# Routing tokens to experts: places per two batches, rows sent in four groups, attention results stored by token

## The reference

```python
x = x + tanh(g_xattn) * attention(layernorm(x), ctx, mask, topk=32)   # 16 heads of 16
x = x + tanh(g_ffn) * moe(layernorm(x))

# moe: 8 experts, 2 choices a token, N = 4096 tokens, capacity = N / 8 * 1.25 = 640
probs = softmax(x_flat @ gate_w.T); top, idx = top_k(probs, 2); top = top / sum(top)
for k in range(2):
    onehot = (idx[:, k, None] == experts)
    pos = (cumsum(onehot, axis=0) - 1)[token, idx[:, k]]     # place among the earlier tokens of that expert
    valid = pos < capacity
    disp[idx[:, k], pos] += x_flat where valid                # a table of its own for each k
    out += where(valid, top[:, k] * expert(disp)[idx[:, k], pos], 0)
```

## Time and profile before

| | |
|---|---|
| median of 3 runs | 3430.61 us (3429.76 to 3431.26) |
| the profiled execution | 3430.36 us, of which the span is 3428.6 us |
| busy, share of the span | PE 80%, DVE 82%, ACT 57%, POOL 53% |
| mean granted TensorE clock | 0.931 |

### The profile page before, as it was taken

The page is one execution under the profiler, slowest core; times in us unless marked ns, Lnnn a source line. Parts: engine busy times, 40 slices in busy tenths (PEclk is TensorE's granted clock), DMA queues, the critical chain, the costliest instruction groups (busy, mean ns, idle before and its releaser), DMA issues. The chain is left out here.

```text
span 3428.6 us, 77423 instructions
## 1 busy us (share of the span) xinstructions
PE 2727.2 (80%) x23469; PEld 1888.0 (55%) x23470; DVE 2805.7 (82%) x20098; ACT 1970.0 (57%) x3382; POOL 1826.1 (53%) x1278
## 2 busy tenths in 40 slices
PE   7838888888888888888888888832713999999990
PEld 5514445454544445454545454521603999999990
DVE  6749999999999999999999999944713766667653
ACT  2228888888888888888888888820200222222220
POOL 1017777777777777777777777710153111111107
PEclk9969999999999999999999999965856999999995
DMA  6961121121121111211211212011222112211206
GB/s 204 253 178 32 32 51 42 32 62 32 32 61 32 44 50 32 62 32 32 62 32 39 55 32 61 3 30 33 92 74 92 55 64 69 69 66 68 67 28 193
DMA packets 141983, 220.41 MB, mean 64 GB/s; under 512 B 22432, under 2 KB 103584, under 8 KB 138496
## 3 DMA queue, kind: packets, MB, share of 16 engines
q1 hardware_dynamic: 116608, 171.43, 18.3%
q0 software_dynamic: 9472, 29.37, 2.8%
q10 hardware_dynamic: 15488, 14.68, 1.3%
HBM read 142.02 MB, written 73.40 MB: 63 GB/s over the span
## 5 line engine op out<-in xcount | busy, mean ns | idle before, releaser
L568 DVE MAX8 a_cand<-a_sc 128x8 f32<-128x43 f32 (+1 forms) x12288 | 1682.8, 201 | 42.8 <-ACT a_sc L506 42.6
L640 POOL TENSOR_SCALAR a_low<-a_sc,a_top 128x1024 bf16<-128x1024 f32 x512 | 1456.2, 2844 | 0.0
L513 ACT ACTIVATE a_ex<-a_ps_e,a_nmax 128x1024 f32<-128x1024 f32 x512 | 577.7, 1128 | 149.4 <-PE a_ps_e L418 149.4
L506 ACT COPY a_sc<-a_ps_s 128x1024 f32<-128x1024 f32 x512 | 531.5, 1038 | 187.5 <-PE a_ps_s L406 170.7
L520 ACT COPY a_exT<-a_ps_t 128x512 f32<-128x512 f32 x1024 | 552.5, 602 | 0.3 <-PE a_ps_t L439 0.3
L439 PEld LDWEIGHTS a_ps_t<-a_ident,a_ex 128*128 128x128 f32 x4096 | 478.2, 140 | 102.1 <-ACT a_ex L513 1.0
L439 PE MATMUL a_ps_t<-a_ident,a_ex 128*128 128x128 f32 x4096 | 529.8, 272 | 0.8 <-ACT a_exT L520 0.8
L427 PE MATMUL a_ps_c<-a_low,a_row_of 128*16 128x512 bf16 x1024 | 307.2, 382 | 255.6 <-POOL a_low L640 214.7
L416 PE MATMUL a_ps_e<-a_ks,a_qs 96*128 96x512 bf16 x1024 | 394.3, 385 | 0.0
L418 PE MATMUL a_ps_e<-a_low,a_lowest 128*128 128x512 bf16 x1024 | 390.1, 381 | 0.0
L1292 POOL TENSOR_TENSOR e_wl<-e_raw,e_wh 128x2048 fp32r<-128x2048 f32 x24 | 110.5, 4603 | 519.9 <-DVE e_wh L1429 519.9
(11 more groups left out here) (196 smaller groups left out, 4676.4 us busy)
## 6 DMA issues: line engine op xcount, KB each, us to landing
scr_v<-p_vp SPq DMA_DIRECT2D x32, 512.0 KB, 6.1
a_vs<-scr_v SPq DMA_DIRECT2D x32, 512.0 KB, 5.8
a_mask<-in_mask SPq DMA_DIRECT2D x32, 512.0 KB, 6.6
scr_k<-p_kp SPq DMA_DIRECT2D x96, 128.0 KB, 2.4
a_ks<-scr_k SPq DMA_DIRECT2D x32, 384.0 KB, 4.7
a_qs<-scr_q SPq DMA_DIRECT2D x192, 64.0 KB, 5.2
scr_disp<-a_zeros SPq DMA_DIRECT2D x32, 320.0 KB, 6.9
e_xin<-scr_disp SPq DMA_DIRECT2D x40, 256.0 KB, 2.7
```

What stands on the lines that cost most here:

```text
L506: nc.scalar.copy(sc[:, i % 4, :], ps_s[:]).then_inc(copied[u], 1)
L513: nc.scalar.activation(ex[:, s % 2, :], ps_e[:], ACT.Exp, bias=nmax[:, v, s:s + 1]).then_inc(expd, 1)
L568: ins = nc.vector.max(c[:, 8 + n:8 + n + 7 * CH + 1:CH], sc[:, i % 4, pl.cut[n]:pl.cut[n + 1]])
L640: nc.gpsimd.tensor_scalar(low[:, i % 2, :], sc[:, i % 4, :], top[:, u, i, pl.TOPK - 1:pl.TOPK], None, ALU.is_lt).then_inc(lowed, 1)
```

## The change

- **Layout.** `attn` is now ordered by token, 32 tiles of 256 columns. `attend` and `repair` write their columns to the place of the head. PE turns the rows straight from `attn`; POOL's `gather` and the buffer `ain` are gone. `norm` writes straight into `xn`, which PE reads too; `keep_rows` and the buffer `xs` are gone, with the waits that belong to them.
- **Places per group.** A group is two batches, 8 tiles. In the steps of batches 2, 4 and 6, DVE marks the group before after `choose` (`mark`), and after `norm` it works out its slots (`slots`). POOL adds the marks tile by tile into a running sum `sofar`, eight dependent additions. PE, at the end of its step, takes the counts within a tile and the sums up to a tile into one accumulation of two products (`places`). The last group follows the last batch.
- **Sends per group.** POOL issues the 16 sends of a group as soon as its slots are there, then waits for the marks of the next group.

```diff
@@ attend, normalise
-                    ins = nc.scalar.activation(attn[:, bass.ds(Gn, 1), j * DK:(j + 1) * DK].rearrange("p o d -> p (o d)"),
+                    ins = nc.scalar.activation(attn[:, Gn // (G * pl.QT) * pl.QT + Gn % pl.QT, (Gn // pl.QT % G * HG + j) * DK:(Gn // pl.QT % G * HG + j + 1) * DK],
@@ repair, tile on DVE
-                link(V.tensor_scalar(attn[:, I * QT + t, bass.ds(j * DK, DK)], ps_u[:, 0:DK], rden[:], None, ALU.mult))
+                link(V.tensor_scalar(attn[:, (I // G) * QT + t, bass.ds((I % G) * (HG * DK) + j * DK, DK)], ps_u[:, 0:DK], rden[:], None, ALU.mult))
@@ route, POOL
-            def gather(b, u, start):
...
-            def keep_rows(b, u):
...
-            pool.wait_ge(slots_done, 2)
-            for n in range(TT):
-                for k in range(K2):
...
+            nc.gpsimd.memset(sofar[:, 0], 0.0).then_inc(added, 1)
+            for g in range(NG):
+                pool.wait_ge(hot, g + 1)
+                for t in range(g * GT, (g + 1) * GT):
+                    pool.wait_ge(added, t + 1)
+                    nc.gpsimd.tensor_tensor(sofar[:, t + 1], sofar[:, t], onehot[:, t], ALU.add).then_inc(added, 1)
+                pool.wait_ge(slots_done, g + 1)
+                for t in range(g * GT, (g + 1) * GT):
+                    for k in range(K2):
+                        pool.indirect_dma_start(
+                            out=scr["disp"], out_offset=bass.IndirectOffsetOnAxis(ap=slot_to[:, t, k:k + 1], axis=0),
+                            in_=xn[:, t, :], in_offset=None, bounds_check=ROWS - 1, oob_is_err=False).then_inc(sent, 16)
             pool.wait_ge(sent, 16 * TT * K2)
@@ route, PE
-                    if t == 0:
-                        pe.wait_ge(a_in, b + 1)
...
-                                                 ain[:, u, t, k * P:(k + 1) * P], ident[:])
+                                                 attn[:, b * QT + t, k * P:(k + 1) * P], ident[:])
...
-                                                 xs[:, u, t, k * P:(k + 1) * P], ident[:])
+                                                 xn[:, b * QT + t, k * P:(k + 1) * P], ident[:])
...
+                if b and b % GB == 0:
+                    places(b // GB - 1)
+
+            def places(g):
+                pe.wait_ge(hot, g + 1)
+                pe.wait_ge(added, g * GT + GT)
+                if g:
+                    pe.wait_ge(picked, g)
+                tiles = slice(g * GT, (g + 1) * GT)
+                nc.tensor.matmul(ps_n[:, 0:GT * C], upto[:], onehot[:, tiles].rearrange("p t k e -> p (t k e)"),
+                                 start=True, stop=False)
+                nc.tensor.matmul(ps_n[:, 0:GT * C], ones[:], sofar[:, tiles].rearrange("p t k e -> p (t k e)"),
+                                 start=False, stop=True).then_inc(counted, 1)
...
-            nc.tensor.matmul(ps_n[:, 0:TT * K2 * E], upto[:], onehot[:].rearrange("p t k e -> p (t k e)"),
...
+            places(NG - 1)
@@ route, DVE
-                if not start:
-                    dve.wait_ge(xn_kept, b - 1)
...
-                    ins = nc.vector.tensor_scalar(xs[:, u, t, :], x1[:, b * QT + t, :], mv[:, u, t, 0:1],
+                    ins = nc.vector.tensor_scalar(xn[:, b * QT + t, :], x1[:, b * QT + t, :], mv[:, u, t, 0:1],
...
                     choose(b - 1, 1 - u, start and b == 1)
+                if b and b % GB == 0:
+                    mark(b // GB - 1)
                 norm(b, u, start)
+                if b and b % GB == 0:
+                    slots(b // GB - 1)
+
+            def mark(g):
+                n = slice(g * GT, (g + 1) * GT)
+                link(nc.vector.tensor_copy(chosen[:, n], which[:, n, 0:K2]))
+                for k in range(K2):
+                    ins = nc.vector.tensor_tensor(onehot[:, n, k, :], lane[:].unsqueeze(1).broadcast_to([P, GT, E]),
+                                                  chosen[:, n, k:k + 1].broadcast_to([P, GT, E]), ALU.is_equal)
+                ins.then_inc(hot, 1)
+
+            def slots(g):
...
+                link(V.tensor_scalar(first[:, n], chosen[:, n], float(K2 * CAP), None, ALU.mult))
+                link(V.tensor_scalar(first[:, n, 1], first[:, n, 1], float(CAP), None, ALU.add))
+                dve.wait_ge(hot, g + 1)
+                dve.wait_ge(counted, g + 1)
+                V.tensor_tensor(flat(place[:]), ps_n[:, 0:GT * C], flat(onehot[:, n]), ALU.mult).then_inc(picked, 1)
+                dve.wait_ge(picked, g + 1)
+                link(V.tensor_reduce(at[:, n], place[:], AX_X, ALU.add))
...
+                V.tensor_copy(slot_to[:, n], tmp[:, n]).then_inc(slots_done, 1)
...
+            mark(NG - 1)
+            slots(NG - 1)
+            V.tensor_copy(slot_from[:], first[:]).then_inc(slots_done, 1)
```

More of the change, by code:

```diff
@@ L876, in route @@
     B, QT, TT, D, E, KD = pl.B, pl.QT, pl.TT, pl.D, pl.E, pl.KD
-    GD = pl.HG * pl.DK
     CAP, K2 = pl.CAP, 2
     ROWS = E * K2 * CAP
+    GB = 2
+    GT = GB * QT
+    NG = B // GB
+    C = K2 * E
     attn, x1, slot_to, slot_from, weight = (keep[n] for n in ("attn", "x1", "slot_to", "slot_from", "weight"))
@@ L913, in route @@
         onehot = sb("r_onehot", [P, TT, K2, E])
-        before = [sb(f"r_before{i}", [P, TT, K2, E]) for i in range(2)]
-        place = sb("r_place", [P, TT, K2, E])
+        sofar = sb("r_sofar", [P, TT + 1, K2, E])
+        place = sb("r_place", [P, GT, K2, E])
         at = sb("r_at", [P, TT, K2])
@@ L929, in route @@
         made = sem("r_made")
-        a_in = sem("r_a_in")
-        xn_kept = sem("r_xn_kept")
         x_in = [sem(f"r_x_in{u}") for u in range(2)]
@@ L947, in route @@
         hot = sem("r_hot")
+        added = sem("r_added")
         counted = sem("r_counted")
@@ L950, in route @@
         e_out = sem("r_e_out")
+        picked = sem("r_picked")
         slots_done = sem("r_slots_done")
@@ L989, in _ @@
                                     pattern=[[1, P]], channel_multiplier=-1).then_inc(made, 1)
-            def gather(b, u, start):
-                if not start:
[L993 to L997, removed]
-            def keep_rows(b, u):
[L1000 to L1010, removed]
-            pool.wait_ge(slots_done, 2)
-            for n in range(TT):
-                for k in range(K2):
-                    pool.indirect_dma_start(
-                        out=scr["disp"], out_offset=bass.IndirectOffsetOnAxis(ap=slot_to[:, n, k:k + 1], axis=0),
-                        in_=xn[:, n, :], in_offset=None, bounds_check=ROWS - 1, oob_is_err=False).then_inc(sent, 16)
+            nc.gpsimd.memset(sofar[:, 0], 0.0).then_inc(added, 1)
[10 more added lines that the diff above has]
+                            in_=xn[:, t, :], in_offset=None, bounds_check=ROWS - 1, oob_is_err=False).then_inc(sent, 16)
             pool.wait_ge(sent, 16 * TT * K2)
@@ L1173, in step @@
                     choose(b - 1, 1 - u, start and b == 1)
+                if b and b % GB == 0:
+                    mark(b // GB - 1)
                 norm(b, u, start)
+                if b and b % GB == 0:
[8 more added lines that the diff above has]
+            def slots(g):
+                V = nc.vector
+                n = slice(g * GT, (g + 1) * GT)
+                flat = lambda ap: ap.rearrange("p t k e -> p (t k e)")
+                link(V.tensor_scalar(first[:, n], chosen[:, n], float(K2 * CAP), None, ALU.mult))
[5 more added lines that the diff above has]
+                link(V.tensor_reduce(at[:, n], place[:], AX_X, ALU.add))
+                link(V.tensor_scalar(valid[:, n], at[:, n], float(CAP), None, ALU.is_le))
+                link(V.scalar_tensor_tensor(out=tmp[:, n], in0=at[:, n], scalar=-1.0, in1=valid[:, n], op0=ALU.add,
+                                            op1=ALU.mult))
+                link(V.tensor_tensor(first[:, n], first[:, n], tmp[:, n], ALU.add))
+                link(V.tensor_scalar(tmp[:, n], valid[:, n], -float(1 << 20), float(1 << 20), ALU.mult, ALU.add))
+                link(V.tensor_tensor(tmp[:, n], tmp[:, n], first[:, n], ALU.add))
+                V.tensor_copy(slot_to[:, n], tmp[:, n]).then_inc(slots_done, 1)
             dve.wait_ge(w_in, 16 * 5)
@@ L1185, in _ @@
             V = nc.vector
[L1186 to L1190, removed]
-            link(V.tensor_tensor(tmp[:, :, 0], best[:, :, 1], best[:, :, 0], ALU.subtract))
-            V.memset(before[0][:, 0:1], 0.0).then_inc(e_in, 1)
@@ L1194, in _ @@
[L1194 to L1209, removed]
-            dve.wait_ge(e_out, 1)
-            link(V.scalar_tensor_tensor(out=tmp[:], in0=at[:], scalar=-1.0, in1=valid[:], op0=ALU.add, op1=ALU.mult))
-            link(V.tensor_tensor(first[:], first[:], tmp[:], ALU.add))
@@ L1213, in _ @@
[L1213 to L1217, removed]
+            mark(NG - 1)
+            slots(NG - 1)
+            V.tensor_copy(slot_from[:], first[:]).then_inc(slots_done, 1)
+            dve.wait_ge(slots_done, NG + 1)
```

(7 more changed lines are left out.)

7 lines of the change are left out of this document (removed).

## The result

The changed kernel takes 3384.9 us, the median of four runs (3382.64 to 3386.18), against 3430.94 us of the kernel before in four runs beside it: a ratio of 0.9863 with a 95% interval of 0.9848 to 0.9878. The prediction said 3386. All medians and ratios here are of fast runs: one run of half_sends (7246.61 us) and one of the kernel before (6633.46 us, beside one_pool) took about twice as long and are left out. The profiled execution took 3385.42 us, its span is 3383.4 us, 45.2 less than the 3428.6 before.

A forecast was written before the change was run, and what follows sets the result against it. POOL's 64 sends, issued alone after the batches, bound the kernel; four rounds of 27.4 us plus 3 x 1.1 from 2433.3 end issue at 2546.2 instead of 2590.2, so 3430.4 − 44 gives 3386 us, range 3376 to 3400.

The forecast's parts named there:

- the first signal: In the routing batches, DVE's first marks are ready for POOL and PE at 2433.3 us.
- the four stretches from signal to first send: In each of POOL's four rounds, additions, count, slots and the start of sending take 6.9 us.
- the four bursts: POOL's 16 sends per round take 20.5 us, plus 1.1 us in the three rounds with batches beside them.
- The sums: Eight dependent additions per group on POOL: 0.35 us each, 2.8 us, bounds 1.5 and 3.9 us.
- The stretch: Sends beside a busy DVE in the batches cost 1.1 us more per 16 sends.
- Rival 1: Sends beside the batches wait for DVE's operations and take 1.66 us each: 15 us more, 3401 us; chance 0.14.
- rival 2: POOL and DVE exclude each other altogether in the batches, a pair takes 45.5 us: slower, 3437 us; chance 0.03.
- The batches' loss: PE stops at the count, delaying the next residual by 6.7 us in batches 2, 4 and 6: 20 us.
- POOL's 2546 ends last: At the end of issue, POOL's chain ends at 2546 us, the batches' at 2542, so only POOL's counts.
- a tie: In the routing stage, a pair of batches takes 27.9 us and POOL's round 28.5 us.
- Taken at nothing: Effects given no time; in the repair, five tiles' register work hides in DVE's 1.5 us waits, under 0.5 us uncovered.
- Rival 3: Short round: additions 1.5 us, no stretch, early PE, batches lose 4.5 us per pair, round under 26: 3376 us; chance 0.11.

The follow-up runs named there:

- half_sends: The changed kernel with only the first choice's sends in groups 0 to 2, 24 of 64 sends left out: 3381.5 us.
- one_pool: The changed kernel with one-batch groups, count and slots a step later, the first six groups' sums on POOL a group ahead, the last two on DVE: 3369.0 us.
- adds_dve: The changed kernel with the eight running sums of each group on DVE behind the marks instead of on POOL: 3380.5 us.
- places_later: The changed kernel with running sums on DVE, marks at the end of a step, and count and slots in the next step: 3376.5 us.
- layout_only: The kernel before with only the new layout by token, places worked out once and all 64 sends at the end: 3431.8 us.
- tail_busy: The changed kernel with 13 unused copies and 8 unused two-input operations on DVE beside the last 16 sends: 3386.28 us in one run.

## Why the prediction was right

**The mechanism and its size.** 48 sends went beside the batches at their old price, 16 stayed, and the end of issue came at 2544.9 us where 2546.2 was forecast. The parts, by the ledger of POOL's chain: the first signal came 3.2 us late (2436.5 for 2433.3); the four stretches from signal to first send took 6.34, 6.18, 6.18 and 6.12 us, 24.8 instead of 27.6; the four bursts 81.4 instead of 85.3; and POOL waited 2.2 us that the forecast had not. 2546.2 + 3.2 − 2.8 − 3.9 + 2.2 = 2544.9. The forecast is better than its terms: by luck, a late start and an added wait cancelled two terms that were too large.

**The sums** (forecast 2.8 us) took 2.4 us, 0.30 each. The rest of the round, 3.8 us from the sums' end to the first send, was forecast as 1.2 + 1.9 + 0.97 = 4.1.

**The stretch** (forecast 0.07 us a send in three bursts) was 1.311 − 1.277 = 0.03 us in the first burst, 0.02 in the second and none in the third. Rival 1, a send at 1.66 us, falls. So does rival 2: it decides at 2.27 us on average, and even back-to-back copies bring a send to 1.455.

**The batches' loss** (forecast 6.7 us in each of three, 20 in all) was 19.0 us, and the residual came 10.85 us after V(2) where 11.35 was forecast. adds_dve and places_later show that 14.5 of it hang on the stop: 3.4 went with the sums on DVE, 11.1 with the count and slots a step later.

**The step that failed** is the second half of the sentence "POOL's 2546 ends last, so the 20 us that the batches lose are no second term". The forecast had called the two chains a tie, and then chose POOL's. POOL did end last, by 1.4 us in round 4. But with 6.2 instead of 6.9 us from signal to first send and almost no stretch, it waited 2.2 us for DVE in round 3, which is a second term, and half_sends shows the batches' chain alone ending within 3 us of POOL's. The 20 us were as much the bound as the sends. The time hardly minded, because both chains end within 3 us; but a reader who believed the sentence would have gone on to shorten the sends, and removing 24 of them outright won about 3 us, while moving the count by one step, with the sums on DVE, won about 8 (4 of them with the sums alone).

**Taken at nothing, and not nothing: the repair.** The forecast hid five tiles of register work in DVE's 1.5 us wait at a tile's start. The work stands elsewhere. The register rows of L865, which writes the piece, and DVE's idle time before it, before and after:

```profile
L865 DVEq FUSED_REGOPS  x10: 199/250/319, 2295.8 to 2391.9; - x10
...
  DVE g_rden L864: 3.1, 5
```

```profile
L865 DVEq FUSED_REGOPS  x15: 52/283/346, 2296.8 to 2394.1; - x15
...
  DVE g_rden L864: 4.1, 5
```

There are five more of them, and in five passes DVE idles 1.0 us longer between the reciprocal of L864 and L865, where no wait for PE covers them; the profile puts this idle time down to L864. From its first operation to its last (L746 to L865) the repair took 137.9 us before, 138.6 in layout_only and 138.9 after, and from 138.2 to 138.9 in all kernels with the new layout. Of the 3.1 us by which V(2) is late, 1.0 is this, 1.0 was there before the repair began (its start lies between 2254.3 and 2257.4 us among these kernels), and 1.1 lies in batch 0, where the products of the output weights took 5.45 us instead of 4.30 at a lower granted clock (below).

**Rival 3** did not come. The sends hardly stretched, as it said, but the sums took 2.4 us where it had 1.5, a round without its wait for DVE's marks took 26.2 to 27.0 us where it had under 26, and PE did not come early: the batches lost 6.3 us per pair, not 4.5. The removal of POOL's copies gave DVE nothing that the time shows, as layout_only tells.

**What holds a send.** The Trainium skill, page "SBUF — State Buffer", section "SBUF: two separate sides", names a port pair that VectorE (DVE) and GpSimd (POOL) share under a lock, held for a whole instruction. VectorE takes it with an operation in a 2-port mode, which a float32 copy within SBUF (the on-chip memory that the tiles lie in) triggers, or, against a GpSimd operation that reads SBUF, with one that has two inputs there; whichever starts first blocks the other. The traces agree as far as the sends go: one that begins while DVE is inside such an operation, 0.1 us or more after its start, ends 0.85 us after that operation's end, unless its usual 0.97 us take it further. So it is in the changed kernel with L1122, which has two inputs in SBUF, and in tail_busy with a copy:

```profile
2445.48 0.48 DVE L1122 SCALAR_TENSOR_TENSOR attn<-r_aO,r_tg,r_xin 128x256 f32<-128x256 f32 x1
2445.59 1.23 POOL L1001 DMA_INDIRECT scr_disp<-r_xn,slot_to  x1 [0.30 <-issue]
```

```profile
2529.00 0.69 DVE L1223 COPY r_aT<-r_xT 128x1024 f32<-128x1024 f32 x1
...
2529.39 1.15 POOL L1001 DMA_INDIRECT scr_disp<-r_xn,slot_to  x1 [0.31 <-issue]
```

The copy ends at 2529.69 and the send at 2530.54. The send of 1.75 us fits too: the first operation of L1225 ends 1.28 us after its start, at 2537.56, and the send at 2538.42. A send that begins just before such an operation is not held: the one at 2526.75, 0.06 us before the first copy, took its usual 0.97 us. Nor is one held that begins in L1121, one of whose two inputs is PE's result and lies outside SBUF: the send at 2447.12 took 0.98 us. DVE loses nothing that shows, for the 13 copies take 0.693 to 0.699 us each.

So the sends walk in step with operations that stand back to back: 1.455 us is two copies (2 x 9.43 / 13 = 1.451), and 1.32 is one operation with two inputs (10.53 / 8 = 1.316). The cost is what is left of the one operation that a send meets: 0.18 us of 1.277 beside the copies, 0.04 beside the operations with two inputs, and on average 0.03 us or less in this stage, where L1122 takes 0.48 us. The step is shown for operations of 0.48, 0.69 and 1.28 us; that it is the port pair which holds the send is the page's reading, and no run here shows it.

## What to carry to other kernels

Issue that stood alone on an idle chip was hidden here at its old price (1.28 us a send), so look first for the stage in which one queue works and the rest waits. Then look at the in-order engine that meets the new wait: a dependent step placed in the same iteration stops it, and the work queued behind it pays; the same step one iteration later left 4.5 of the 19.0 us here. When two chains are forecast within a few us, say that both bind and test it by taking one's work away, since the sum alone can come out right for either.

## What was not expected of the hardware

- The clock of TensorE in batch 0 differed between two kernels that do the same work there, after the same idle time (8.4 and 8.5 us for a load). The products of the output weights of batch 0, in before and then in after:

```profile
2401.40:2405.70 4.30, 4.30 (x19) 3.70 (x19) 1.48 (x4) 1.87 (x2) 0.00 (x0) 0.86 0.04 13
```

```profile
2403.35:2408.80 5.45, 5.45 (x19) 4.49 (x19) 1.49 (x4) 1.87 (x2) 0.00 (x0) 0.68 0.03 10
```

  Both stretches begin at the lower level (1.2 GHz, 0.50 in these rows) and end at the higher (2.4 GHz, 1.00). PE works without a pause from its first transposes, and the clock rose 3.0 us after them before (at 2402.6) and 5.3 us after them in the changed kernel (at 2406.9). Why it rose later in one was not tried.
- A send lands up to 5.3 us after its issue when x is stored and loaded beside it, against 2.6 at most before. Nothing waits for a single landing, so it cost nothing here.
- A chain of eight small additions on POOL takes 0.30 us each, of which 0.225 (the median) is the operation.
